# Routing the first batch of a two-layer transformer block inside the attention's last heads

## What is computed

```python
x = x + layernorm(attn(layernorm(x)))      # causal, relative position bias, logits / 64
x = x + layernorm(moe(layernorm(x)))
# moe: shared = gelu(x @ Wfc_s + bfc_s) @ Wproj_s + bproj_s
#      probs = softmax(x @ Wr); top 2 of 8, their shares scaled to sum 1
#      routed = sum over the two experts e of share * (gelu(x @ Wfc[e] + bfc[e]) @ Wproj[e] + bproj[e])
```

## Time and profile before

| | us |
|---|---|
| median of 3 executions | 793.37 |
| lowest and highest | 790.54, 797.84 |
| the profiled execution | 791.7 |
| its span in the trace | 790.0 |

### The profile page before, as it was taken

One profiled execution on the slowest core, in us unless ns is written; L12 is line 12 of the kernel. 1 busy time (PEld: TensorE's weight loads), 2 busy tenths in 40 slices (PEclk: granted clock), 3 DMA queues, 4 the chain that ended last, 5 costly groups with the idle time before them and its releaser, 6 DMA issues.

```text
span 790.0 us, 17201 instructions
## 1 busy us (share of the span) xinstructions
PE 692.7 (88%) x4466; PEld 611.2 (77%) x4466; DVE 625.8 (79%) x1663; ACT 551.8 (70%) x1305; POOL 336.0 (43%) x417
## 2 busy tenths in 40 slices
PE   4977999999999999999999999999966457899930
PEld 4856888888888888888888889888865345899920
DVE  5665888889888898888888888888888616788836
ACT  2355888788888888888887888888824314787823
POOL 2548644243433434334333343342353770155543
PEclk9998999999999999999999999999997768999985
DMA  8693643546436465364553644546200247599723
GB/s 296 244 299 71 167 130 85 150 89 167 129 74 163 87 156 137 71 159 100 143 137 83 160 111 118 137 93 161 88 2 1 80 131 224 197 349 367 268 82 112
DMA packets 82050, 114.85 MB, mean 145 GB/s; under 512 B 42496, under 2 KB 59392, under 8 KB 79584
## 3 DMA queue, kind: packets, MB, share of 16 engines
q1 hardware_dynamic: 79232, 108.71, 49.8%
q0 software_dynamic: 2496, 5.15, 1.8%
q10 hardware_dynamic: 288, 0.59, 0.3%
HBM read 48.32 MB, written 32.56 MB: 102 GB/s over the span
## 4 chain that ended last, share of the span: by engine, by line
PE 72%; DVE 8%; issue 6%; another core or an unknown queue 4%; DMA 3%; ACT 3%; POOL 3%; SPq 1%; ACTq 0%; DVEq 0%; POOLq 0%
PE out_ps L1513 17%; PE score_ps L1480 16%; PE trans_ps L1495 16%; PE shared_ps L1527 7%; PE shared_ps L1388 2%; DVE pT_lo L1335 2%; PE shared_ps L1390 2%; PE shared_ps L1389 2%; PE score_ps L1390 2%; PE score_ps L1388 2%; PE score_ps L1389 2%; DVE stats L1016 1%; PE trans_ps L1388 1%; POOL y_scratch L746 1%
## 5 line engine op out<-in xcount | busy, mean ns | idle before, releaser
L832 ACT ACTIVATE probs<-score_ps,row_min 128x128 f32<-128x128 f32 (+7 forms) x256 | 190.1, 743 | 54.4 <-DVE row_min L1088 54.0
L853 ACT ACTIVATE pT_hi<-trans_ps 128x512 fp32r<-128x512 f32 (+3 forms) x384 | 185.3, 492 | 45.7 <-PE trans_ps L1495 34.1
L1101 DVE TENSOR_TENSOR pT_lo<-trans_ps,pT_hi 128x512 fp32r<-128x512 f32 (+3 forms) x384 | 201.7, 552 | 17.8 <-ACT pT_hi L853 17.6
L1088 DVE CUSTOM_DVE_ANT_0 score_ps<-score_ps,bias 128x128 f32<-128x128 f32 (+7 forms) x256 | 194.6, 760 | 26.6 <-PE score_ps L1480 23.3
L1495 PE MATMUL trans_ps<-ident,probs 128*128 128x128 f32 x1152 | 191.1, 275 | 3.2 <-DVE pT_lo L1101 1.8
L1480 PE MATMUL score_ps<-k_hl,q_hl 128*128 128x512 f32 (+2 forms) x768 | 182.9, 352 | 7.2 <-DMA k_hl<-k_hl 5.6
L640 POOL TENSOR_TENSOR acc<-acc,head_out 128x512 f32<-128x512 f32 x64 | 82.8, 1294 | 222.0 <-DVE head_out L1121 221.9
L1495 PEld LDWEIGHTS trans_ps<-ident,probs 128*128 128x128 f32 x1152 | 137.6, 141 | 27.5 <-DVE pT_lo L1101 11.9
L1513 PE MATMUL out_ps<-pT_hi,v_hl 128*128 128x512 f32 (+2 forms) x384 | 156.8, 409 | 1.1 <-DVE pT_lo L1101 1.1
L1480 PEld LDWEIGHTS score_ps<-k_hl,q_hl 128*128 128x128 f32 x768 | 134.9, 189 | 27.7 <-DMA k_hl<-k_hl 5.8
L1513 PE MATMUL out_ps<-pT_lo,v_hl 128*128 128x512 f32 (+2 forms) x384 | 133.3, 347 | 0.0
(11 more groups left out here) (252 smaller groups left out, 1168.3 us busy)
## 6 DMA issues: line engine op xcount, KB each, us to landing
q_hl<-k_hl SPq DMA_DIRECT2D x64, 256.0 KB, 3.7
k_hl<-k_hl SPq DMA_DIRECT2D x32, 512.0 KB, 4.4
v_raw<-v_scratch SPq DMA_DIRECT2D x32, 256.0 KB, 4.6
split_scratch<-normed_rows SPq DMA_DIRECT2D x16, 512.0 KB, 5.3
k_hl<-split_scratch SPq DMA_DIRECT2D x16, 512.0 KB
rows_scratch<-wv SPq DMA_DIRECT2D x16, 455.0 KB, 6.6
v_scratch<-probs SPq DMA_DIRECT2D x12, 512.0 KB, 5.1
normed_rows<-in_W_halves SPq DMA_DIRECT2D x16, 256.0 KB, 4.2
```

Of the source, the lines that this page charges most:

```text
L832: act.activation(probs[s % 4][:, 0:n], scores_of(s % QB)[:, 0:n], ACT.Exp, bias=row_min[:, s:s + 1], scale=-1.0, accum_out=row_sum[:, s:s ...
L853: act.activation(pT_hi[c][:, CH * g:CH * g + m, q * P:(q + 1) * P], trans_ps[k % 2][:, 0:m * P].rearrange("p (m q) -> p m q", q=P), ACT.Co ...
L1088: dve.tensor_tensor_reduce(out=ps, in0=ps, in1=bias_b[b][:, T - n:T], scale=1.0, scalar=3e38, op0=ALU.add, op1=ALU.min, accum_out=row_min[ ...
L1101: dve.tensor_tensor(pT_lo[c][dst], trans_ps[k % 2][:, 0:m * P].rearrange("p (m q) -> p m q", q=P), pT_hi[c][dst], ALU.subtract).then_inc(p ...
```

## The change

- **Order of the heads.** The last twelve heads run batch by batch (`unit`, `F = 4`). Head slots 4 to 9 do batch 0 of heads 4 to 15, two heads in each, and head slots 10 to 15 do batch 1. The projection weights are split twice in each of them, in slots 5 and 13. The loop covers heads 1 and 2 alone; the others are straight code.
- **Batch 0 is routed in the slots of heads 10 to 15.** `early_slot` counts them from 0 to 95 and `route_early(z)` puts a piece behind slot z, on each engine: moments, root, residual, moments, root, offset, one block's normalisation a slot (41 to 49), transposes (52, 60), logits (68), picks (69 to 82), ranks (84), slots (85 to 87), and 13 of batch 0's 16 scatters in slots 88 to 95. Sums and products that DVE made are GpSimd's here, a sum over eight is three halvings. The three remaining scatters stand behind slot 95.
- **Batch 1** is routed behind the attention in two groups of four blocks (`PICKS`), 8 scatters each.
- **The shared expert's weights** are two more halves for `split_half` (18 in place of 16; heads 5 and 6 have two). They are loaded from memory in the last head. PE computes the hidden units of batch 0 right behind the attention; ACT takes the first four gelus before it normalises batch 1.
- **Logits** take 16 columns of weights instead of 256.
- **Row order.** A tile's row pair lies together in one partition (1040 bytes instead of two pieces of 520). Token numbers are counted so that the y arrays come back in pieces of 2048 bytes instead of 512.

The core of the diff:

```diff
+    LAST = 12
+    F = H - LAST
+    P0 = F + LAST // B
+    SCATTERS = {88: 2, 89: 2, 91: 2, 92: 2, 93: 2, 94: 2, 95: 1}
+    EARLY = sum(SCATTERS.values()) - QB
+    PICKS = [(0, QB), (QB, QB + CH), (QB + CH, NB)]
+    def unit(h, b):
+        if isinstance(h, int) and h >= F:
+            i = B * (h - F) + b
+            return F + i % LAST, i // LAST
+        return h, b
 # all engines
-            with pe.Fori(1, H - 1) as h:
+            with pe.Fori(1, F - 1) as h:
                 for s in range(S):
                     slot(h, s, True, False)
-            for s in range(S):
-                slot(H - 1, s, True, True)
+            for h in range(F - 1, H):
+                for s in range(S):
+                    slot(h, s, True, h == H - 1)
 # SP
-                    lo = k * B * T + c * W
-                    sp.dma_start(y_part[k][:, CH * c:CH * (c + 1), :],
-                                 y_dram[lo:lo + W, :].rearrange("(t p) d -> p t d", p=P)).then_inc(y_loaded[c], 16)
+                    src = bass.AP(y_dram.tensor, (k * B * T + CH * c) * D, [[NB * D, P], [D, CH], [1, D]])
+                    sp.dma_start(y_part[k][:, CH * c:CH * (c + 1), :], src).then_inc(y_loaded[c], 16)
 # GpSimd
+            def slots_of(i):
+                pool.wait_ge(ranks_taken, 1)
+                pool.wait_ge(before_ready, 1)
+                then_wait(pool.tensor_tensor(place_of[:, early, :], place[:, early, :], pick[i][:, early, :], ALU.mult))
+                sums = place_of[:, early, :]
+                then_wait(pool.tensor_tensor(sums[:, :, 0:4], sums[:, :, 0:4], sums[:, :, 4:8], ALU.add))
+                then_wait(pool.tensor_tensor(sums[:, :, 0:2], sums[:, :, 0:2], sums[:, :, 2:4], ALU.add))
+                then_wait(pool.tensor_tensor(slot_f[i][:, early].unsqueeze(2), sums[:, :, 0:1], sums[:, :, 1:2], ALU.add))
+            def route_early(z):
...
+                if z in (21, 27):
+                    add_residual(int(z == 27))
+                if z == 71:
+                    less_top()
+                if z in (73, 78):
+                    order_top(int(z == 78))
+                if z == 76:
+                    remove_first()
+                if z == 82:
+                    add_picks()
+                    sum_taken()
+                if z in (86, 87):
+                    slots_of(z - 86)
+                for n in range(SCATTERS.get(z, 0)):
+                    k = sum(m for y, m in SCATTERS.items() if y < z) + n
+                    dispatch(0, k // QB, k % QB)
-            root(1, 0, QB)
+            for t in range(EARLY, QB):
+                dispatch(0, 1, t)
             for s in range(S, TAIL):
                 if s in WO_SLOT:
                     if WO_SLOT[s] == (B - 1, NC - 1):
+                        root(1, QB, QB + CH)
                         pool.wait_ge(oT_psum, H * B * NC - 1)
                     add_head(H - 1, *WO_SLOT[s])
-            root(2, 0, QB)
-            root(1, QB, NB)
-            split_wfc()
-            split_wproj()
-            root(2, QB, NB)
-            dispatch(0)
-            dispatch(1)
+            root(1, QB + CH, NB)
+            name_rows(1)
+            root(2, QB, QB + CH)
+            root(2, QB + CH, NB)
+            for g in range(1, len(PICKS)):
+                for i in range(2):
+                    for t in range(*PICKS[g]):
+                        dispatch(g, i, t)
 # ACT
+            hidden_units(0, 0)
+            normalise_moe_in(QB, QB + CH)
+            nT_evac(1, NC)
+            copy_rows(1)
+            exp_logits(1)
+            normalise_moe_in(QB + CH, NB)
+            nT_evac(1, NC + 1)
+            copy_rows(2)
+            exp_logits(2)
 # DVE
                 if s in WO_SLOT:
-                    if s == max(WO_SLOT):
-                        add_normed(0)
                     scale_head(H - 1, *WO_SLOT[s])
-            moments(x_sb, 0, QB)
+                    if WO_SLOT[s] == (B - 1, 0):
+                        dve.wait_ge(acc_added, H * B * NC - 1)
+                        moments(acc, QB, QB + CH)
...
+            add_normed(QB, QB + CH)
             dve.wait_ge(acc_added, H * B * NC)
-            moments(acc, QB, NB)
+            moments(acc, QB + CH, NB)
+            moments(x_sb, QB, QB + CH)
+            add_normed(QB + CH, NB)
+            scale_and_offset(2, QB, QB + CH)
+            moments(x_sb, QB + CH, NB)
+            scale_and_offset(2, QB + CH, NB)
+            nT_evac(1, NC)
+            take_logits(1)
+            choose(1, 0)
+            choose(1, 1)
+            share(1)
+            find_slots(1)
+            nT_evac(1, NC + 1)
+            take_logits(2)
...
+            find_slots(2)
             find_tiles()
 # PE
-            keep_busy(56)
-            for c in range(NC):
-                transposes(1, c)
-            logits(0)
-            pe.wait_ge(wfc_ready, 1)
+            pe.wait_ge(shared_w_loaded, 32)
             hidden_units(0, 0, 0)
-            keep_busy(16, trans_ps[0])
-            ranks(0)
+            hidden_units(0, 1, 0)
+            keep_busy(32, trans_ps[1])
+            transposes(1, NC)
```

More of the change, by code:

```diff
@@ new lines, in slot @@
+            def slot(h, s, carried, last):
+                row_minimum(h, s)
+                if s >= LAG_DVE:
+                    split_lo(h, s - LAG_DVE)
+                elif carried:
+                    split_lo(h - 1, s - LAG_DVE + S)
+                for slots, do in ((PV_SLOT, invert_sums), (WO_SLOT, scale_head)):
+                    if s in slots:
+                        do(h, *slots[s])
+                    if carried and s + S in slots:
+                        do(h - 1, *slots[s + S])
+                if s in QK_SLOT:
+                    nxt, b, half = QK_SLOT[s]
+                    if not (nxt and last):
+                        split_qk_lo(h + nxt, b, half)
+                route_early(early_slot(h, s))
@@ L1550, in fillers, with logits @@
                 return pieces
+            def logits(g):
+                if g == 0:
+                    pe.wait_ge(wr_ready, 1)
+                else:
+                    pe.wait_ge(oT_ready, H * B * NC)
+                    pe.wait_ge(logit_taken, g)
+                lo, hi = PICKS[g]
+                for t in range(lo, hi):
+                    for part in (nT_hi, nT_lo):
+                        last = pe.matmul((out_ps if g else shared_ps)[:, 2 * E * t:2 * E * (t + 1)], part[:, t * P:(t + 1) * P],
+                                         wr_hl[:], start=part is nT_hi, stop=part is nT_lo)
+                last.then_inc(logit_psum, 1)
@@ new lines, in ranks @@
+            def ranks(g):
+                end = g == len(PICKS) - 1
+                lo, hi = PICKS[g][0] * E, (PICKS[g][1] + end) * E
+                pe.wait_ge(picks_ready, g + 1)
+                if g == 0:
+                    pe.wait_ge(tables_ready, 1)
+                else:
+                    pe.wait_ge(wo_scaled, H * B * NC)
+                    pe.wait_ge(ranks_taken, g)
+                    pe.wait_ge(before_ready, g)
+                pe.matmul(shared_ps[:, lo:hi], before_me[:], taken[:, lo:hi], start=True, stop=False)
+                blocks = (hi - lo) // E
+                for d in range(1, blocks):
+                    last = pe.matmul(shared_ps[:, lo + d * E:hi], ones[:], taken[:, lo:hi - d * E], start=False,
+                                     stop=g == 0 and d == blocks - 1)
+                if g:
+                    last = pe.matmul(shared_ps[:, lo:hi], ones[:], taken_before[g - 1][:].unsqueeze(1).broadcast_to([P, blocks, E]),
+                                     start=False, stop=True)
+                last.then_inc(rank_psum, 1)
@@ new lines, in route_early @@
+            def route_early(z, h, s, last):
+                if z in (52, 60):
+                    wait_shared(h, s, last)
+                    transposes(1, int(z == 60))
+                if z in (54, 62):
+                    pe.wait_ge(nT_ready, NCH + 1 + (z == 62))
+                if z == 68:
+                    wait_shared(h, s, last)
+                    logits(0)
+                if z == 70:
+                    pe.wait_ge(logit_taken, 1)
+                if z == 84:
+                    wait_shared(h, s, last)
+                    ranks(0)
+                if z == 86:
+                    pe.wait_ge(ranks_taken, 1)
@@ L1562, in slot @@
                     piece()
+                route_early(early_slot(h, s), h, s, last)
             for r in range(2):
```

645 lines of the change are left out of this document (385 added, 260 removed).

## The result

The kernel after took 784.8 us at the median (783.2 to 787.7) against 795.6 for the kernel before beside it: ratio 0.989, interval 0.985 to 0.994, so 1.1% faster where 2.1% had been forecast. Two more sets gave 0.989 (0.987 to 0.991) and 0.991 (0.988 to 0.994). In all three the kernel before took 792 to 796 us; the two further sets ran on one chip. On three other chips it takes 773 to 774 us, and on one of these, where the kernel after ran too, it is *slower*: 777.3 against 773.6, ratio 1.0048 (1.0026 to 1.0069). That is the larger finding.

A forecast was written before the change was run, and what follows sets the result against it. PE bounds attention and tiles; between them routing, 32 scatters and a stalled shared expert take roughly 90 us. Tail -21.2, inserted pieces +5.5, unrolling +0.5, y -1.0 sum to -16.2: 777 us against the median of 793.4, range 765 to 789.

The forecast's parts named there:

- GpSimd in the last half head: Attention's end: 16 scatters precede batch 1's first-half add, which ends at 586.1 instead of starting at 580.71; about 4 us late.
- The tail's scatters: Behind the attention: 16 scatters left instead of 32, first at 608.9, last ending at 629.1 instead of 651.8.
- The tail's gain: Attention's end to first tile: 21.2 us gained; bounds 30 without a stall and 14.
- the 21.0 us of DVE's work: Tile table to first tile: 19.0 us of DVE's own work plus 2 us of last transposes and evictions.
- the stall of 10.8 us: Tail after the change: engines wait behind the scatters from 622.3 to 633.1, with 8.6 us lost.
- What the stall cost before: Table to first tile: 46.5 us less 21.0 of work, so 25.5 lost over a 32.6 us stall put down to no engine.
- the third rival: Attention's end: stall comes there too, 13.4 us into its scatters; 8 us more than GpSimd's delay, 785 in all; chance 0.11.
- The attention: Heads 10 to 15: batch 0's inserted routing costs 5.5 us, near PE's 3.8, since DVE's and ACT's idle time takes most.
- a head above 34 us: Sign of being wrong: head period above 34 in heads 10 to 15; 32.5 to 33.5 would be right.
- The unrolling: Attention: twelve of fourteen loop iterations become straight code, costing 0.5 us for all, from -1 to +5.
- The end: Return of y in 2 KB pieces instead of 512 B: gains 1.0 us (0 to 2.5).
- slower: Whole kernel: chance 0.03 of being slower than before, bound 801.3 us; faster 0.74, same 0.23.

The follow-up runs named there:

- run 3: Kernel after with batch 0's three scatters that followed the attention's last slot moved behind GpSimd's last sums and roots; ratio to before 1.0011, before 773.
- run 4: Kernel after with all 16 scatters of batch 0 behind GpSimd's last sums and roots ("all behind"); ratio to before 0.9984, before 773.
- run 16: Kernel after with batch 0's 16 scatters laid into GpSimd's idle gaps, once more; ratio to before 0.9972, on a chip where before takes 772.6 us.
- run 18: Kernel after unchanged, on a chip where before takes 773.6 us ("after, before 773"); ratio to before 1.0048.
- run 10: Kernel after with batch 0's 16 scatters laid into GpSimd's idle gaps; ratio to before 0.9892, before 791.6.
- run 12: Kernel before without its 32 scatters, on a chip where before takes 791.6 us; table ends at 625.03, first tile at 651.0.
- run 1: Kernel before with heads 3 to 14 taken out of the loop, nothing else changed; ratio 1.0067, 5.2 us slower, before 773.
- run 9: Kernel after unchanged, on a chip where before takes 791.6 us; ratio to before 0.9911.
- run 7: Kernel after with the routing's matrix instructions in heads 13 to 15 issued twice, 32 more; attention 5.0 us longer, before 792.1.
- run 8: Kernel after with DVE's 16 statistics and 16 aggregates for batch 0 in heads 10 to 12 issued twice; those heads 2.1 us longer.
- the pauses: Kernel before with GpSimd additions behind each of the first three groups of eight scatters (1.0107, again 1.013) or behind every scatter (807.0 us).
- runs 5 to 12: Two sets of four: before unchanged, after unchanged (twice), variants of after, and before without scatters; the kernel before took 792.1 and 791.6 us.
- run 11: Kernel after with all 16 scatters of batch 0 behind GpSimd's last sums and roots, once more; ratio to before 1.0023, before 791.6.
- run 14: Kernel before with one GpSimd addition (1.3 us) behind every scatter; 807.0 us, before 772.6.

## Where the prediction was right and where it failed

The clock of before plus 13 us (the attention's growth) is the clock to compare with.

**GpSimd in the last half head: right.** Sum of batch 1 forecast from 584.8 to 586.1; measured 598.00 - 13 = 585.0. The 4 us that it is late are on the path, as said. What I did not see is that they could be had back: the scatters stood ahead of the sums by choice, and on chips of the 773 kind 3 to 6 us lie in that order (runs 3, 4 and 16 against 18); on the other kind run 10 gained 1 us, inside the noise.

**The tail's scatters: right.** First at 608.9, last until 629.1; measured 609.2 and 630.3. The pace of 1.265 us was a little short: over the whole row of before it is 1.30.

**The tail's gain: right in size, by errors that cancel.** Forecast 21.2; from the last row minimum to the first tile it was 101.9 before and is 79.4 now, 22.5 less. But the 21.0 us of DVE's work from table to first tile were too few: without any stall, and with no scatter to wait for, this stretch takes 26.0 (run 12), 26.6 (all behind, before 773) and 26.7 (after, before 773), for PE, ACT and DVE take turns in it. And the stall of 10.8 us that I put into the tail of after, with 8.6 lost, isn't there: from the table (636.1) to the first tile are 25.9 us, as without one. What is left is one wait of 2.3 to 3.0 us ahead of the table, which ended at 636.12 - 13 = 623.1 and not at 620.9. The stall that isn't there put my 21.2 too low by 8.6 us, the work and the table put it too high by 4.9 and 2.2: that it came close is luck.

**What the stall cost before: too high in the prediction.** I took all of 46.5 - 21.0 = 25.5 us. With the same 32 scatters and no stall the stretch takes 30.8 us (run 1), so the stall cost 15.7; the rest is work, and the wait for the rows of the last scatter, which I had left out. Of the 22.5 us that the tail gained, 15.3 are thus the stall's (101.9 before, 86.6 in run 1), and 7.1 are what the change brings without one (86.6 in run 1, 79.5 in run 18).

**Where the stall went.** It came in the attention's end, the third rival's place: DVE waits 5.1 us for a remote releaser, from 591.94 on, 19 us behind the first scatter and 10 us into the second group of them. But it cost nothing there. The sum of batch 1 begins 15.4 us behind the last row minimum both with it (597.97, run 9) and without it (599.31, run 18): GpSimd's own row of scatters hides it. Rival three's price, 8 us, was wrong, though its total, 785, is the time that came out; that is luck.

**The attention: the step that failed.** I had 5.5 us for the inserted pieces, within 3.8 to 17.8, and 0.5 for the straight code; measured 9.4, and 3.4 to 3.8. Together 13.2 instead of 6.0; this 7 us, less the 1.3 that the tail gained more, is the miss at the first tile (8.5 to 9.6 earlier, forecast 15.2). PE's term was right: 3.8 forecast, 3.5 measured, 0.11 us for an instruction (run 7). What failed is the step behind it, that idle time of DVE and ACT (12% and 17%) would take all but 1.7 us of their 14. It took little more than half: 9.4 - 3.5 = 5.9 us were paid, of which some 2.1 are the moments' (run 8). By head, 2.9 of them came in heads 10 to 12, where PE has nothing inserted, and 2.2 in head 13 beside the eight transposes. I had named a cause, that the slots are a round trip PE to ACT to DVE, and priced it too low; that it is the cause is argued, not shown. I had written that a head above 34 us would refute me: heads 10, 12, 13 and 14 are.

**The unrolling** I bounded at -1 to +5 and placed near the lower end, because nothing spoke for a price. One row did: the straight head 15 saved 0.25 us only, though two projections were gone. It cost 3.0 to 3.4 us in the attention. The Trainium skill (Runtime: NRT & Kernel Launch, Instruction fetch mechanics) says that kernels prefer full unrolling where possible, since a branch can stall on a fetch; run 1 says the opposite here, +5.2 us.

**The end.** 1.0 us forecast for the larger pieces of y; DVE waited 8.46 us for them after 9.09, but 9.5 to 10.0 in three other traces of the kernel after, and from the last scatter of a tile to the end it is 26.3 after 26.2. Nothing.

**The sum again**, at the first tile: 13.2 - 22.5 = -9.3, and the medians of the whole say -6 to -11. On a chip without the stall: 13.2 less 7.1 (86.6 in run 1, 79.5 in run 18), +6 at the first tile, +3.8 at the end; the 2 us between the two are not placed, for the kernel before as it is has no trace on such a chip. No rival had that, because all were worked out from one chip's trace; "slower" had 0.03.

**Open.** What sets the stall off. It needs scatters (run 12) and a certain kind of chip; one row of 32 brings a wait of 16.1 us, 16 spread over 37 us bring one of 1.6, which fits a dense row as its cause, but the pauses that would have told density from number never met such a chip. Nor is it known what differs between the chips, or how common the 792 kind is: runs 5 to 12 were all on one such chip.

## What to carry to other kernels

A gain that comes from removing a stall which the profile can't put down to any engine is a gain on that chip: run the kernel before on another chip first, for the same code lost 0.5% there. Work put into a loop that keeps its main engine full costs that engine's whole part and here about two fifths of everybody else's, and straight code in place of a loop has its own price. On an in-order queue such as GpSimd's, issue what others wait for first, and put transfers that nobody awaits yet into the gaps behind it.

## What the runs showed of the hardware

- With indirect scatters in a row, one kind of chip stops PE, DVE and ACT for a whole stretch of 8 us at DMA share 0.15 (run 11); another doesn't, with the same instructions (run 4). In the tile phase the first kind also takes 176 to 184 ns for a packet of 4 KB (means from the first tile to the last scatter, ten traces), the second 170 to 174 (the nine traces with all weights), and this phase lasts 91.6 to 97.5 us instead of 86.5 to 88.7.
- TensorE's clock can fall inside a loop that keeps it busy: to 0.50 for 3.4 us in run 7, at a cost of 1.5 us. A price that is read from such a run has to be freed of it first.
- In run 14, GpSimd adds 128x512 tiles between the scatters, and DVE's small steps beside it slow down fourfold on average. DVE's group there, and one of its four with GpSimd's addition beside it:

```profile
L1243 DVE TENSOR_TENSOR pick<-rank,top 128x64 f32<-128x64 f32 x4 | 4.0, 999 | 0.1
616.74 1.76 DVE L1243 TENSOR_TENSOR pick<-rank,top 128x64 f32<-128x64 f32 x1
617.36 1.05 POOL L744 TENSOR_TENSOR idle<-idle 128x512 f32<-128x512 f32 x1
```

and with pauses behind every eighth scatter only:

```profile
L1243 DVE TENSOR_TENSOR pick<-rank,top 128x64 f32<-128x64 f32 x4 | 0.9, 225 | 0.1
```

The tile table ended at 639.7 instead of 626.4. The Trainium skill (SBUF — State Buffer, SBUF: two separate sides) says that one of the two holds the shared port for its whole instruction and the other waits. These rows agree in that: the ten long ones from 616 to 640 take 1.4 to 1.8 us, and each ends 0.1 us or less behind the end of an addition (618.50 behind 618.41). But the page gives the port to the one that starts first, and by its record this DVE instruction started 0.6 us ahead of the addition. In the prediction I had weighed this rule at 0.5 us; a kernel that moves steps to GpSimd has to weigh it per instruction.
